# Routed blocks of the first half of the tokens moved ahead in both expert stages, and gate and up biases folded into a plane of the activations

## The chip, the cores and the metric

One core of a Trainium2 chip runs the whole program: TensorE (PE), VectorE (DVE), ScalarE (ACT), GpSimd (POOL) and SyncE (SP, which here only issues DMAs). The metric is the time of one execution on the device in microseconds, the median of several runs.

## What is computed

Four layers over the same 2048 tokens of 128 features, each a token mixer and then a feed-forward part. What matters here are the two expert layers, the first and the last, with two of the experts chosen for every token. Cut from the reference of the last one:

```python
d2 = jnp.sum(xs * xs, -1, keepdims=True) + jnp.sum(centroid * centroid, -1)[None, :] - 2.0 * (xs @ centroid.T)
w, sel = jax.lax.top_k(jnp.sqrt(jnp.maximum(d2, 1e-12)), 2)      # 8 experts
w = jax.nn.softmax(w, axis=1)
for e in range(8):                                                # Wg, W1: 128 x 342, W2: 342 x 128
    h = silu(xs @ Wg[e] + bg[e]) * (xs @ W1[e] + b1[e])
    out = out + we[:, e:e + 1] * (h @ W2[e] + b2[e])
```

`xs` is layernormed without gain or bias, so the sum of a token's 128 features is 0. The first expert layer has 7 routed experts and a shared one that all tokens pass, of width 352, without biases; its router is a plain product. All weights are float32; every product is made of three (high x high, high x low, low x high parts).

## The kernel before

**Stages.** The program is a row of stages with a barrier of all engines between them (`Stage.release`, L165): attention of layer 0, experts of layer 0 (184.8 to 384 us of the profile), attention and `selected_ffn` of layer 1, the same of layer 2, and a last stage (944.8 to the end) that holds the channel attention of layer 3 and its experts. Both expert stages are made by `experts`, the last with `by_distance` true. Tokens lie in 16 tiles of 128, four tiles to a run, four runs.

**Routing.** For each run the stage normalises x (`stats`, `norm`), makes router scores (`router`, `score`), picks two experts for each token (`one_hot`), and numbers the rows of every expert with matmuls of ones (`ranks` on PE, `spot` on DVE): this gives each of a token's two copies a row in `rows` in DRAM, where every expert has its own region. `send` on POOL writes the rows there with indirect DMAs (L1200), two to a tile, eight to a run, 64 in the two stages; all count on one semaphore, `rows_sent`. When all four runs are through, the event `map` makes the block table: PE counts the rows of each expert (L1879), and DVE's `block_table` (L1438 to L1459) turns this into a list of blocks of 128 rows, 38 in the first stage and 39 in the last, each with its expert and its place in `rows`. SP waits for all of `rows_sent` and for the table, reads one entry per block (L1156) and loads the block into one of 8 buffers `yb` (L1159).

**Slots.** A block is worked off in slots that overlap: PE transposes the block two slots ahead (`turn`, L1782), makes gate and up (`gate_up`: L1793, L1794, L1797, each for gate and for up, and in the last stage L1796 for the biases), transposes h (`turn_h`, L1808) and multiplies by the down weights (`down`: L1820, L1821, and L1824 for the down bias). ACT makes silu and the high parts, DVE the product and the low parts, POOL adds the result's rows into `acc` in DRAM (L1207). A slot has 19 matmuls in the last stage and 16 in the first. `work` is the order of the blocks: in the first stage shared tiles 0 to 13, routed blocks 0 to 37, shared tiles 14 and 15; in the last stage only routed blocks. What stands between the slots, and in which order, is a list written by hand that all engines walk through: `shared_first_events` and `mixed_events`. In the last stage all of the channel attention (events that begin with c_) and the routing stand ahead of the first slot.

**Biases of the last stage.** SP zeroes a tile `bias` of 128 x 6496 from DRAM (L2858, 3248 KB) and then places the high and low parts of all biases in its first two partitions; a matmul against a tile of ones in those partitions adds them (L1796, L1824).

**Weights of the last stage.** `load_experts` is called by `load_last` at the end of SP's work in `selected_ffn` of layer 2: gate and up weights of the 8 experts, 128 partitions (L908), three DMAs of down weights (L911: twice 128 partitions, and the rest of 342 rows, 86), then the zeros of `bias`. In the last stage ACT copies them to their high parts and DVE takes the low ones (event `split`, 2 + 2 + 4 experts behind steps 4, 5 and 6 of the list).

## Time and profile before

| | us |
|---|---|
| median of 3 runs | 1178.87 |
| lowest and highest | 1174.91, 1188.52 |
| profiled execution | 1187.66 |
| its span in the profile | 1185.9 |
| its mean granted clock of TensorE | 0.902 of full speed |
| PE busy | 955.9 (81%) |
| DVE, ACT, POOL busy | 719.0, 572.6, 463.9 |
| experts of layer 0 | 184.8 to 384 |
| last stage | 944.8 to 1185.9 |
| its stream of routed slots | 1056.5 to 1160.3 |

The profile shows one execution. A row of a timeline gives the start, the busy time, the engine and line, out<-in by the program's names, and in brackets how long the engine was idle before it and who released it. "SPq" are DMA issues of SP, with the time that the issue took SP, not the transfer. In a row of stretches come the stretch, its length, then for PE, PE's weight loads, DVE, ACT and POOL the busy time with the number of instructions, the granted clock of TensorE as a share of full speed, the busy share of the core's 16 DMA engines and what they moved.

### The profile page before, as it was taken

What the parts mean: (1) busy time and instruction counts of PE and PEld (TensorE: products, weight loads), DVE (VectorE), ACT (ScalarE), POOL (GpSimd) and SP (SyncE); (2) the same over time, 40 slices, a digit from 0 to 9 for tenths busy, and PEclk for the clock granted to TensorE, in tenths of its full rate; (3) what the DMA queues carried; (4) which work ended last, traced back from release to release, by engine and by line L of the source; (5) the groups of instructions that cost most, each with busy time, mean ns of one, the idle gap of its engine ahead of it and who ended that gap; (6) DMA issues with size and microseconds to landing.
All of it is one profiled execution on the core that took longest, in us unless ns stands there. A gap on an engine that the chain in (4) does not pass through costs nothing. (4 is left out here: it accounts for less than half of the span.)

```text
span 1185.9 us, 24279 instructions
## 1 busy us (share of the span) xinstructions
PE 955.9 (81%) x8086; PEld 754.2 (64%) x8101; DVE 719.0 (61%) x1952; ACT 572.6 (48%) x1193; POOL 463.9 (39%) x528
## 2 busy tenths in 40 slices
PE   6899884769993888897789999999997775139990
PEld 5566664769993655555666677767676654139990
DVE  4678645556665767773657666676635556735554
ACT  2577651325553466764444544454432533325552
POOL 1266664533444221211341333343443515733332
PEclk8899995779996999999999999999998887559995
DMA  8121110111212021111400101111113600111113
GB/s 283 49 66 50 50 52 10 35 43 43 55 45 76 26 68 56 56 57 40 139 19 2 32 9 37 38 37 38 38 38 91 237 2 18 33 40 49 53 44 107
DMA packets 80904, 67.05 MB, mean 57 GB/s; under 512 B 6753, under 2 KB 73592, under 8 KB 80402
## 3 DMA queue, kind: packets, MB, share of 16 engines
q1 hardware_dynamic: 76274, 57.04, 16.9%
q0 software_dynamic: 4512, 8.47, 2.2%
q8 instruction: 70, 1.15, 0.4%
q14 instruction: 48, 0.39, 0.1%
HBM read 39.30 MB, written 26.58 MB: 56 GB/s over the span
## 5 line engine op out<-in xcount | busy, mean ns | idle before, releaser
L454 DVE TENSOR_REDUCE a_rowmax<-a_banks 128x4 f32<-128x1024 f32 (+1 forms) x112 | 136.8, 1222 | 64.2 <-PE a_banks L721 28.1
L2314 POOL TENSOR_TENSOR a_both<-a_probs 128x512 f32<-128x512 f32 x64 | 86.2, 1347 | 159.9 <-ACT a_probs L2539 159.9
L576 ACT ACTIVATE a_probs<-a_banks 128x1024 f32<-128x1024 f32 x112 | 114.9, 1026 | 59.9 <-PE a_banks L707 47.2
L1207 POOL DMA_INDIRECT acc<-m_result,m_yb x77 | 75.5, 981 | 141.3 <-DVE m_result L1498 74.4
L2539 ACT ACTIVATE a_probs<-a_banks 128x1024 f32<-128x1024 f32 x64 | 65.6, 1025 | 88.5 <-PE a_banks L2598 88.5
L1607 ACT ACTIVATE m_gate<-m_banks 128x352 f32<-128x352 f32 (+1 forms) x93 | 42.9, 462 | 99.3 <-PE m_banks L1797 97.5
L2445 DVE TENSOR_REDUCE a_rowmax<-a_banks 128x4 f32<-128x1024 f32 x64 | 78.0, 1219 | 13.4 <-PE a_banks L2575 13.4
L1200 POOL DMA_INDIRECT rows<-m_yrow,m_idx x64 | 65.7, 1027 | 51.4 <-issue 21.8
L2612 PE MATMUL a_banks<-a_probs,a_V 128*64 128x256 f32 x512 | 69.4, 392 | 0.6 <-ACT a_craw L2528 0.6
L1478 DVE TENSOR_TENSOR m_h<-m_banks,m_gate 128x342 f32<-128x342 f32 (+1 forms) x55 | 28.5, 517 | 66.4 <-ACT m_gate L1607 59.9
L1820 PE MATMUL m_banks<-e_down,m_hT_hi 128*128 (+2 forms) x231 | 63.6, 344 | 1.0 <-DVE m_result L1498 1.0
L360 POOL TENSOR_SCALAR_AFFINE_SELECT a_probs<-a_probs 128x512 f32<-128x512 f32 (+1 forms) x48 | 38.5, 803 | 64.9 <-ACT a_probs L576 64.8
L749 PE MATMUL a_banks<-a_probs,a_V 128*32 128x256 f32 x720 | 58.4, 396 | 6.8 <-ACT a_raw L564 6.3
L1793 PE MATMUL m_banks<-e_gu_hi,m_y_hi 128*128 x154 | 56.7, 368 | 2.8 <-issue 0.8
L707 PE MATMUL a_banks<-a_QT,a_KT 25*128 25x256 f32 x384 | 48.5, 327 | 12.2 <-DVE a_rowmax L454 10.9
L1484 DVE TENSOR_TENSOR m_hT_lo<-m_banks,m_hT_hi 128x384 fp32r<-128x384 f32 x93 | 51.1, 550 | 4.6 <-ACT m_hT_hi L1613 4.2
L1821 PE MATMUL m_banks<-e_down,m_hT_lo 128*128 (+2 forms) x231 | 51.4, 223 | 0.0
L707 PEld LDWEIGHTS a_banks<-a_QT,a_KT 25*128 25x128 f32 x384 | 29.7, 184 | 33.9 <-issue 20.1
L1797 PE MATMUL m_banks<-e_gu_hi,m_y_lo 128*128 x154 | 50.1, 326 | 0.0
L1808 PE MATMUL m_banks<-ident,m_h 128*128 128x128 f32 (+2 forms) x279 | 48.2, 284 | 2.3 <-DVE m_hT_lo L1484 2.1
L1794 PE MATMUL m_banks<-e_gu_lo,m_y_hi 128*128 x154 | 50.0, 325 | 0.0
L721 PE MATMUL a_banks<-a_KT,a_QT 24*128 24x256 f32 x384 | 48.8, 332 | 0.9 <-ACT a_KT L588 0.9
(378 smaller groups left out, 2812.1 us busy)
## 6 DMA issues: line engine op xcount, KB each, us to landing
rows<-fill SPq DMA_DIRECT2D x16, 520.0 KB, 4.5
a_factor<-recip_rows SPq DMA_DIRECT2D x28, 256.0 KB, 4.8
rows<-fill SPq DMA_DIRECT2D x15, 455.0 KB, 4.2
m_yb<-rows SPq DMA_DIRECT2D x77, 65.0 KB, 1.8
f_expert<-in_experts SPq DMA_DIRECT2D x16, 257.5 KB, 2.9
m_parts<-acc SPq DMA_DIRECT2D x16, 256.0 KB, 4.9
bias<-in_bias_zero SPq DMA_DIRECT2D x1, 3248.0 KB, 20.7
e_gu_lo<-in_gu SPq DMA_DIRECT2D x1, 2736.0 KB
```

The lines of the kernel that those rows point to most:

```text
L454: nc.vector.reduce_max(o, src, AX).then_inc(rowmax_ready, 1)
L576: nc.scalar.activation(probs[h][:, k, :, :], ps[:, 4:6, :], ACT.Exp, scale=SCALE).then_inc(exp_done, 1)
L707: last = mm(ps[:, 4 + x_, b * SEQ:(b + 1) * SEQ], kk[rows, 2 * gp + b, kt * P:(kt + 1) * P], q[rows, 2 * gp + b, :], start=True, stop=True)
L749: last = mm(o[:, 0:SEQ], v, probs[h][:, b // 2 + (0 if causal else 2 * kt), jj, (b % 2) * SEQ:(b % 2 + 1) * SEQ], start=kt == 0, stop=kt = ...
L1200: nc.gpsimd.indirect_dma_start(rows.rearrange("n p c -> (n p) c"), bass.IndirectOffsetOnAxis(idx[:, c:c + 1], 0), yrow[k][:, r * RT + t, : ...
L1207: nc.gpsimd.indirect_dma_start(acc.rearrange("k n d -> (k n) d"), bass.IndirectOffsetOnAxis(yb[b % YB][:, P:P + 1].bitcast(U32), 0), resul ...
L1793: mm(o, y_hi[i % 3][:, :], gu_hi[:, s], start=True, stop=False)
L1820: mm(both, hT_hi[i % 2][0:r, c, :], part[0:r, c, :, :], start=c == 0, stop=False)
L2314: nc.gpsimd.tensor_tensor(both[u % 4][:, :, :], p[:, :, 0, :], p[:, :, 1, :], ALU.add).then_inc(both_ready, 1)
L2445: nc.vector.reduce_max(rowmax[i1 % 2][:, :, j, :, n].rearrange("p t h -> p h t"), ps[:, b:b + 2, :].rearrange("p h (t k) -> p h t k", t=T) ...
L2539: nc.scalar.activation(probs[u % 4][:, :, :, :].rearrange("p h t q -> p h (t q)"), ps[:, 4:6, :], ACT.Exp, scale=SCALE).then_inc(exp_done, 1)
L2612: last = mm(ps[h * D64:(h + 1) * D64, 6, 0:SEQ], V[i % 3][:, kt, j, :], probs[b][:, h, kt, :], start=kt == 0, stop=kt == T - 1)
```

## The change

**Early blocks.** `rows_sent` becomes two semaphores, for runs 0 and 1 and for runs 2 and 3. After run 1's ranks the counts so far are known; DVE's new event `early` makes a table of the first `early_blocks(layer)` blocks, 10 in the first stage and 9 in the last, of those blocks that are full with rows of the first half of the tokens. The event `map` (`late_table`) makes the table of the others, from the counts of all and what the early ones took. SP loads the early blocks after the first semaphore and the early table, the others after the second of each. The count matmuls stand in `ranks` of runs 1 and 3 now. In the first stage the order is shared 0 to 9, routed 0 to 9, shared 10 to 13, routed 10 to 37, shared 14 and 15, and `early` stands behind `router` 2; in the last stage `early` stands behind step 5 of the list, and `map` behind the fourth slot entry. The buffers `yb` and `result` grow from 8 and 4 to 12 each.

**Bias plane.** Since the features of a normalised token sum to 0, its last feature is minus the sum of the others, and the product with a weight matrix is that of 127 features with the matrix less its last row. So feature 127 of the sent rows is set to 1.0, row 127 of the gate and up weights holds the biases, and from every other row the last row is subtracted. This takes away the two L1796 matmuls of a slot, and adds eight tensor_tensor of 128x684 on POOL (`less_last`), a tile `last_row` of 128 x 5472 that is loaded from DRAM (127 copies of the last rows, and zeros), and a DMA of the biases into partition 127. `bias` keeps the down biases alone: 128 x 1024. The events of ACT's copies (`high`) and of DVE's differences (`split`) are now apart and each is placed by itself in the list. ACT's table for silu is loaded at `gap` 3.

```diff
@@ load_experts
-    eng.dma_start(w["gu_lo"][:, :, :].bitcast(F32), src_gu[0:n, :, :].rearrange("e p f -> p e f")).then_inc(w["loaded"], 16)
+        eng.dma_start(w["gu_lo"][0:P - 1, :, :].bitcast(F32),
+                      src_gu[0:n, 0:P - 1, :].rearrange("e p f -> p e f")).then_inc(w["loaded"], 16)
+        eng.dma_start(w["gu_lo"][P - 1:P, :, :].bitcast(F32), bias_gu).then_inc(w["loaded"], 16)
+        eng.dma_start(w["last_row"][:, :, :], copies.rearrange("p (e f) -> p e f", e=n)).then_inc(w["loaded"], 16)
@@ expert_weights
-    w["parts"] = 16 + 16 * FC
+    w["parts"] = (16 if n < NE else 48) + 16 * FC
@@
+def early_blocks(layer):
+
+    return -((ROUTED[layer] * (P - 1) - TOKENS) // P)
@@ mixed_events
-    events = [("c_stats", 0), ("c_norm", 0)]
-    splits = {4: [0, 1], 5: [2, 3], 6: [4, 5, 6, 7]}
+    events = [("c_stats", 0), ("less_last", 0), ("less_last", 1), ("c_norm", 0), ("high", 0), ("high", 1)]
+    highs = {("c_zn", 0): [2, 3], ("norm", 0): [4, 5], ("norm", 1): [6, 7]}
+    splits = {("c_norm", 1): [0, 1], ("c_shift", 0): [2, 3], ("c_shift", 1): [4], ("c_shift", 2): [5], ("c_shift", 3): [6],
+              ("score", 3): [7]}
+    less_last = {("c_stats", 1): [2, 3, 4, 5], ("c_out", 0): [6, 7]}
...
+        if k == 5:
+            events += [("early", 0)]
+    events += [("send", RUNS - 1, 3)]
+    slots = range(-2, W + 2)
+    return events + [("slot", s) for s in slots[:4]] + [("map", 0)] + [("slot", s) for s in slots[4:]]
@@ experts
-            work = [("shared", t) for t in range(14)] + [("routed", b) for b in range(NB)] + [("shared", 14), ("shared", 15)]
+            work = ([("shared", t) for t in range(FIRST_SHARED)] + [("routed", b) for b in range(EARLY)]
+                    + [("shared", t) for t in range(FIRST_SHARED, 14)] + [("routed", b) for b in range(EARLY, NB)]
+                    + [("shared", 14), ("shared", 15)])
@@ SP
-            sp.wait_ge(rows_sent, 16 * 2 * TILES)
-            sp.wait_ge(map_ready, 1)
+            sp.wait_ge(rows_sent[0], 16 * TILES)
+            sp.wait_ge(early_map, 1)
             own_wait(sp, st.sp_waited)
             for b in range(NB):
+                if b == EARLY:
+                    sp.wait_ge(rows_sent[1], 16 * TILES)
+                    sp.wait_ge(late_map, 1)
+                    own_wait(sp, st.sp_waited)
@@ POOL
+                if kind == "less_last":
+                    pool.wait_ge(w["loaded"], w["parts"])
+                    raw_gu, _, _ = raw_parts(w, layer, r)
+                    nc.gpsimd.tensor_tensor(raw_gu, raw_gu, w["last_row"][:, r, :], ALU.subtract).then_inc(less_last, 1)
@@ DVE
+            def early_table():
+                then(nc.vector.memset(step[:, :], float(TILES)))
+                then(nc.vector.reduce_sum(count[:, :], more[:, :, :], AX))
+                block_table(0, EARLY, 0.0, early_map)
+                then(nc.vector.tensor_scalar(taken[:, :], last_of[:, :], float(EARLY), None, ALU.min))
+                nc.vector.tensor_copy(done[:, 0:1], taken[:, 0:1])
+                then(nc.vector.tensor_tensor(done[:, 1:NE], taken[:, 1:NE], taken[:, 0:NE - 1], ALU.subtract))
@@ ACT
-                act.wait_ge(w["loaded"], w["parts"])
...
+                act.wait_ge(less_last, e + 1)
@@ PE, gate_up
-                    if by_distance:
-                        mm(o, bias_one[:, :], biases[:, e, s], start=False, stop=False)
@@ PE, slots
+                    if r == -2 and by_distance:
+                        pe.wait_ge(spot_ready, RUNS)
-                    if r == first_routed - 1:
+                    if r == first_early - 1:
...
-                        pe.wait_ge(map_ready, 1)
+                        pe.wait_ge(early_map, 1)
+                        own_wait(pe, pe_waited)
+                    if r == first_late - 1:
+                        pe.wait_ge(late_map, 1)
@@ load_last
-            load_experts(sp, 3, a["gu3"], a["down3"], w3)
+            load_experts(sp, 3, a["gu3"], a["down3"], w3, (a["gu_last"], a["bias_gu"]))
             sp.dma_start(g.bias[:, :].bitcast(F32), a["bias_zero"]).then_inc(g.bias_zeroed, 16)
```

SP at the end of `selected_ffn` of layer 2 and the start of the last stage, before (e_gu_lo: gate and up weights, e_down: down weights, m_bias_raw: the biases of the last stage):

```order
339 L1972 DMA f_expert<-in_experts 128x515
340 L908 DMA e_gu_lo<-in_gu 128x8x684
341 L911 DMA e_down<-in_down 128x8x128 x2
342 L911 DMA e_down<-in_down 86x8x128
343 L2858 DMA bias<-in_bias_zero 128x6496
344 L1924 UNCONDITIONAL_BRANCH
345 L1144 UNCONDITIONAL_BRANCH
346 L1147 DMA m_bias_raw<-in_bias 32x203
347 L1151 DMA bias<-m_bias_hi 1x32x203
```

And after, at the same place:

```order
339 L2045 DMA f_expert<-in_experts 128x515
340 L913 DMA e_gu_lo<-in_gu 127x8x684
341 L915 DMA e_gu_lo<-in_bias_gu 1x5472
342 L916 DMA e_last_row<-in_gu_last 128x5472
343 L919 DMA e_down<-in_down 128x8x128 x2
344 L919 DMA e_down<-in_down 86x8x128
345 L2931 DMA bias<-in_bias_zero 128x1024
346 L1997 UNCONDITIONAL_BRANCH
347 L1178 UNCONDITIONAL_BRANCH
348 L1181 DMA m_bias_raw<-in_bias 32x32
```

The load of gate and up has 127 partitions in place of 128, two loads stand behind it, and the zeros are 128x1024 in place of 128x6496.

PE at the start of the last stage's slots, after the change (m_chosen: the choices of all runs, m_yb: a loaded block, m_y_hi and m_y_lo: the parts of its transpose):

```order
3108 L1844 MATMUL m_banks<-m_chosen,m_ones 128x8 x4
3109 L1857 MATMUL m_banks<-ident,m_yb 128x128 x2
3110 L1906 TENSOR_LOAD m_block_map
3111 L1906 ISA x2
3112 L1868 ISA
3113 L1868 MATMUL m_banks<-e_gu_hi,m_y_hi 128x342
3114 L1869 REGISTER_ALU
3115 L1869 MATMUL m_banks<-e_gu_lo,m_y_hi 128x342
3116 L1870 MATMUL m_banks<-e_gu_hi,m_y_lo 128x342
```

Before, the same place had L1796 between L1794 and L1797 for gate and again for up.

DVE in the last stage, after the change, behind the choice of run 3's experts (m_top_atf: the experts chosen; e_gu_lo and e_down: the split of one expert; m_step to m_block_map: the early table):

```order
1207 L1420 CAST m_top_atf<-m_top_at 128x8
1208 L1341 TENSOR_TENSOR e_gu_lo<-e_gu_lo,e_gu_hi 128x684
1209 L1342 TENSOR_TENSOR e_down<-e_down 128x2x128
1210 L1343 TENSOR_TENSOR e_down<-e_down 86x128
1211 L1515 MEMSET m_step 1x8
1212 L1516 TENSOR_REDUCE m_count<-m_more 1x8
1213 L1498 TENSOR_TENSOR m_upto<-m_before,m_count 1x64
1214 L1499 TENSOR_REDUCE m_last_of<-m_upto 1x8
1215 L1500 TENSOR_TENSOR m_past<-m_number_f,m_last_of 1x72
1216 L1505 TENSOR_REDUCE m_of_block<-m_past 1x9
```

Before, two splits stood here, four more behind them ahead of the slots, and the whole table behind those; now one split and the early table stand here, and the late table stands between slots.

## Rows read from the trace of the kernel before

**Rows 1.** A stretch of the last stage: busy us by engine, granted clock, DMA share, GB/s.
```profile
1080.00:1150.00 70.00, 70.00 (x525) 69.21 (x525) 40.32 (x112) 37.69 (x110) 26.90 (x28) 1.00 0.19 52
```

**Rows 2.** TensorE's timeline: start, busy us, line, tiles, idle before and its releaser.
```profile
1034.79 0.27 PE L1879 MATMUL m_banks<-m_chosen,m_ones 128*128 128x8 bf16 x4 [2.26 <-DVE m_spot_f L1427]
1054.49 0.47 PE L1782 MATMUL m_banks<-ident,m_yb 128*128 128x128 f32 x1 [19.43 <-DMA m_yb<-rows]
...
1056.54 0.65 PE L1793 MATMUL m_banks<-e_gu_hi,m_y_hi 128*128 x1 [0.34 <-issue]
```

**Rows 3.** The chain of waits, last stage: start, us, what.
```profile
1049.23 2.40 DMA rows<-m_yrow,m_idx
...
1066.19 0.15 PE m_banks L1796
...
1066.61 0.33 PE m_banks L1808 x3
...
1147.70 0.33 PE m_banks L1808 x3
```

**Rows 4.** TensorE's timeline, first stage, at its first routed slots.
```profile
254.47 0.33 PE L1782 MATMUL m_banks<-ident,m_yrow 128*128 128x128 f32 x1 [1.80 <-issue]
...
261.82 0.45 PE L1782 MATMUL m_banks<-ident,m_yb 128*128 128x128 f32 x1 [3.57 <-DMA m_yb<-rows]
```

**Rows 5.** POOL's timeline, last stage.
```profile
948.12 1.02 POOL L1188 TENSOR_TENSOR m_c_in_rstd<-m_c_in_var,minus_half 128x4 f32<-128x4 f32 x1 [2.40 <-DVE m_c_in_var L1284]
...
962.66 1.01 POOL L1188 TENSOR_TENSOR m_c_in_rstd<-m_c_in_var,minus_half 128x4 f32<-128x4 f32 x1 [9.19 <-DVE m_c_in_var L1284]
...
1022.81 0.96 POOL L1200 DMA_INDIRECT rows<-m_yrow,m_idx  x1 [0.30 <-issue]
```

**Rows 6.** VectorE's timeline, first stage and last.
```profile
217.76 0.53 DVE L1478 TENSOR_TENSOR m_h<-m_banks,m_gate 128x352 f32<-128x352 f32 x1 [2.66 <-ACT m_gate L1607]
...
249.76 0.27 DVE L1438 TENSOR_TENSOR m_more<-m_banks,m_limit_f 1x128 f32<-1x128 f32 x1
...
253.62 0.16 DVE L1459 TENSOR_SCALAR m_block_map<-m_of_block 1x38 int32<-1x38 f32 x1
...
1028.45 0.87 DVE L1296 TENSOR_TENSOR e_gu_lo<-e_gu_lo,e_gu_hi 128x684 fp32r<-128x684 f32 x1
...
1031.09 0.28 DVE L1390 TENSOR_TENSOR m_one_hot<-w_moe,m_top_atf 128x32 bf16<-128x32 f32 x2
```

**Rows 7.** Stretches of the first stage.
```profile
261.80:266.50 4.70, 4.67 (x21) 4.61 (x21) 1.16 (x4) 1.56 (x5) 0.00 (x0) 0.50 0.27 61
275.00:355.00 80.00, 77.73 (x556) 73.50 (x555) 49.68 (x137) 45.09 (x139) 33.74 (x35) 1.00 0.19 51
```

**Rows 8.** A group of the page: line, op, shape, count, busy us, mean ns.
```profile
L2314 POOL TENSOR_TENSOR a_both<-a_probs 128x512 f32<-128x512 f32 x64 | 86.2, 1347 | 159.9 <-ACT a_probs L2539 159.9
```

**Rows 9.** Stretches of the two weight loads: last columns clock, DMA share, GB/s.
```profile
24.00:27.00 3.00, 3.00 (x12) 2.21 (x12) 2.18 (x7) 0.00 (x0) 1.45 (x3) 0.50 1.22 266
922.00:925.00 3.00, 2.47 (x15) 2.02 (x14) 1.82 (x10) 2.05 (x7) 2.07 (x3) 1.00 1.02 405
930.00:935.00 5.00, 3.57 (x18) 2.78 (x18) 3.67 (x15) 2.70 (x7) 4.17 (x7) 1.00 0.14 40
939.00:944.00 5.00, 4.91 (x44) 4.71 (x42) 0.68 (x1) 1.58 (x4) 2.63 (x4) 0.99 1.01 437
```

**Rows 10.** SP's timeline: DMA issues, us that each took SP.
```profile
914.78 0.43 SPq L908 DMA_DIRECT2D e_gu_lo<-in_gu  x1
915.27 11.09 SPq L911 DMA_DIRECT2D e_down<-in_down  x3
926.41 8.78 SPq L2858 DMA_DIRECT2D bias<-in_bias_zero  x1
```

**Rows 11.** All engines at the start of the last stage.
```profile
944.83 0.17 POOL L1176 IOTA m_place<- 128x32 int32 x1 [2.84 <-POOLq L165]
```

**Rows 12.** DMA issues of the page: KB each.
```profile
e_gu_lo<-in_gu SPq DMA_DIRECT2D x1, 2736.0 KB
```

More of the change, by code:

```diff
@@ L951 @@
 TOKENS = TILES * P
+FIRST_SHARED = 10
 ROW = P + 2
-BIAS = NE * (2 * F_EXP[3] + P)
+BIAS = NE * P
 BIAS_ROWS = 32
@@ L979, in shared_first_events @@
               ("send", 0, 2), "slot", ("router", 1), ("stats", 3), ("send", 0, 3), ("score", 1), ("norm", 2), "slot",
-              ("gap", 1), ("one_hot", 1), "slot", ("spot", 1), ("share", 1), ("send", 1), ("router", 2), "slot",
-              ("score", 2), ("norm", 3), "slot", ("gap", 2), ("one_hot", 2), "slot", ("spot", 2), ("share", 2),
+              ("gap", 1), ("one_hot", 1), "slot", ("spot", 1), ("share", 1), ("send", 1), ("router", 2), ("early", 0),
+              "slot", ("score", 2), ("norm", 3), "slot", ("gap", 2), ("one_hot", 2), "slot", ("spot", 2), ("share", 2),
               ("send", 2), ("router", 3), "slot", ("score", 3), "slot", ("gap", 3), ("one_hot", 3), "slot",
@@ L988, in mixed_events @@
 def mixed_events(W):
-    events = [("c_stats", 0), ("c_norm", 0)]
-    splits = {4: [0, 1], 5: [2, 3], 6: [4, 5, 6, 7]}
+    events = [("c_stats", 0), ("less_last", 0), ("less_last", 1), ("c_norm", 0), ("high", 0), ("high", 1)]
[3 more added lines that the diff above has]
+    less_last = {("c_stats", 1): [2, 3, 4, 5], ("c_out", 0): [6, 7]}
+    extra = (("less_last", less_last), ("high", highs), ("split", splits))
     for k in range(RUNS + 3):
@@ L998, in mixed_events @@
                 ("send", d, 2)]
-        events += [e for e in step if 0 <= e[1] < RUNS]
-        events += [("split", e) for e in splits.get(k, [])]
-    events += [("send", RUNS - 1, 3), ("map", 0)]
-    return events + [("slot", s) for s in range(-2, W + 2)]
+        for e in step:
+            if 0 <= e[1] < RUNS:
+                events += [e] + [(name, s) for name, at in extra for s in at.get(e, [])]
+        if k == 5:
[3 more added lines that the diff above has]
+    return events + [("slot", s) for s in slots[:4]] + [("map", 0)] + [("slot", s) for s in slots[4:]]
 def experts(nc, g, layer, key, w, mix=None, bias=None, out=None):
@@ L1043, in experts @@
         count = st.sb("count", [1, NE])
+        before = st.sb("before", [1, NE, NE])
         upto = st.sb("upto", [1, NE, NE])
-        last_of = st.sb("last_of", [1, NE])
+        last_of, taken, done, step = (st.sb(n, [1, NE]) for n in ("last_of", "taken", "done", "step"))
         past = st.sb("past", [1, NB, NE])
-        of_block = st.sb("of_block", [1, 4, NB])
+        of_block = st.sb("of_block", [1, 2, NB])
         block_map = st.sb("block_map", [1, 2, NB], I32)
@@ L1101, in experts @@
                  "fn_ready", "x_done", "pe_waited"))
+        rows_sent = [st.sem(f"rows_sent{k}") for k in range(2)]
         block_loaded = [st.sem(f"block_loaded{k}") for k in range(YB)]
@@ L1126, in experts @@
                    ("combine", 3), ("shift", 2), ("residual", 1), ("shift", 3), ("residual", 2), ("residual", 3)]
-        split_at = {e[1]: n + 1 for n, e in enumerate(e for e in events if e[0] == "split")}
         bank = 4 if by_distance else 7
@@ L1461, in low_y, with late_table @@
+            def late_table():
+                nc.vector.tensor_scalar(step[:, :], done[:, :], -1.0, float(TILES), ALU.mult, ALU.add)
+                then(nc.vector.reduce_sum(count[:, :], more[:, :, :], AX))
+                nc.vector.tensor_tensor(step[:, 0:NE - 1], step[:, 0:NE - 1], done[:, 1:NE], ALU.add)
+                then(nc.vector.tensor_tensor(count[:, :], count[:, :], done[:, :], ALU.subtract))
+                block_table(EARLY, NB, done[:, 0:1], late_map)
             def low_y(i):
@@ L1579, in _, with high @@
             nc.scalar.preload_act_table(ACT.Exp if by_distance else ACT.Silu)
-            def split(e):
+            def high(e):
                 r = rows_of[2]
@@ L1681, in _ @@
                         nc.scalar.activation(th[r % 2][:, :], gap[r % 2][:, :], ACT.Tanh, scale=0.5).then_inc(th_ready, 1)
-                if kind == "split":
-                    split(r)
-                if kind == "map" and by_distance:
+                if kind == "high":
+                    high(r)
+                if kind == "gap" and r == RUNS - 1 and by_distance:
                     nc.scalar.preload_act_table(ACT.Silu)
@@ L1769, in ranks @@
                               stop=a == G - 2)
+                if r in (HALF - 1, RUNS - 1):
+                    for q in range(r + 1):
+                        last = mm(counted, ones[:, :], chosen[q][:, :], start=q == 0, stop=q == r)
                 last.then_inc(rank_ps, 1)
@@ L1875, in _ @@
                     ranks(r)
-                if kind == "map":
-                    pe.wait_ge(spot_ready, RUNS)
-                    for q in range(RUNS):
-                        last = mm(counted, ones[:, :], chosen[q][:, :], start=q == 0, stop=q == RUNS - 1)
-                    last.then_inc(count_ps, 1)
                 if kind == "slot":
-                    if r == first_routed - 1:
+                    if r == -2 and by_distance:
+                        pe.wait_ge(spot_ready, RUNS)
+                    if r == first_early - 1:
                         if by_distance:
```

106 lines of the change are left out of this document (64 added, 42 removed).

## The prediction

> **What bounds the kernel now.** I read the page first: TensorE is busy for 81% of the span, but that is a mean over stages with different limits, so the views by stretch decide. In the stream of routed slots of the last stage, 1080 to 1150, TensorE is busy for 70.00 of 70 us at the full clock [rows 1]: every matmul there is time. Ahead of that stream it waits. Its own timeline [rows 2] shows 19.43 us idle before the first transposes of `m_yb`, released by the DMA from `rows`, and the chain of waits [rows 3] says what that DMA waited for: the last of POOL's indirect sends of run 3 (start 1049.23), 2.40 us until its rows had landed. The first stage has the same gap in small: 3.57 us before 261.82, behind 1.80 us in which the block table is made [rows 4].
>
> **Early blocks, last stage.** POOL's sends come eight to a run. Run 1's last starts at 1022.81 [rows 5]; with the 2.40 us to landing of the chain, `rows_sent[0]` is complete at 1025.2. The early table stands on VectorE behind the scores of run 3. At that place stand two splits before, from 1028.45 to 1031.09, 1.32 us each [rows 6]. After, it is one split and fifteen small operations, the first twelve of them up to the map. The whole table of the first stage, thirteen operations up to its map, took 4.0 us (249.76 to 253.78, same rows); the early one works on 9 blocks, and I take 3.0, with 2.4 and 4.0 as bounds. So the early map is there at 1028.45 + 1.32 + 3.0 = 1032.8. From the landing of the sends (1049.23 + 2.40 = 1051.63) to TensorE's first transposes at 1054.49, SP's reads and the load took 2.86 us, so block 0 is there at 1035.7. TensorE waits as well for `spot` of run 3, done near 1034.8, where its count matmuls start; the small operations slip it by less than 1. First turn at 1035.8, first gate matmul 2.05 later, as before (1054.49 to 1056.54), hence 1037.8: a gain of 18.7 us (bounds 16 to 20).
> The second half of the sends ends as before, and its first block can be in SBUF when block 0 was, at 1054.5. It is wanted nine slots of 2.25 us behind the first, its gate matmuls at 1058 and its transposes one to two slots sooner, 1054 to 1057. That is close, and I charge 0.3.
>
> **Bias plane.** Two of nineteen matmuls of a slot go. In a full stretch each of them (L1796) moves the chain on by 0.15 to 0.16 us [rows 3]. The pace: from the transposes at 1066.61 to those at 1147.70 it is 81.09 us for 32 slots, 2.534 each; less 0.31 is 2.22. The bound from the other side is the first stage, whose slots have no such matmul: 556 matmuls in 80 us at 16 a slot are 35 slots, 2.287 each with their gaps and with 352 columns in place of 342 [rows 7]. I take 2.25: 39 x 0.284 = 11.1 us (9.7 to 12.2), and 0.5 more for the first two slots, at the half clock, where each step is twice as long.
>
> **Late tables.** They stand in the stream of slots now. In the first stage the table cost TensorE 1.80 us of idling, and it goes on doing so. In the last stage it stood where TensorE idled anyway; now I charge the same 1.8 there, bounds 0 and 3.7 (the whole table less a slot's slack).
>
> **First stage.** The 3.57 us stall should go, since ten early blocks stand before the late ones, and with it part of the half clock: in the stretch behind it the granted clock is 0.50 for 4.7 us [rows 7], 2.3 us lost, and about 1 more before the stall; I give half of it, 1.65. The early table takes 3 us of VectorE near a gap of 2.66 (before 217.76, [rows 6]): 0.5 lost, and as much again where shared blocks meet the later runs of the router. Gain 3.57 + 1.65 - 1.0 = 4.2, bounds 1 to 7.
>
> **What the plane adds on POOL.** Eight subtractions of 128 x 684. The nearest row has 1347 ns for 128 x 512 [rows 8], 2.6 ns an element, so 1.80 us each. Two stand behind the first `c_in_rstd`, the next four have the gap of 9.19 us before 962.66 [rows 5], two come later: hidden, 0 to 0.2. `high` and `split` only move into idle places of ScalarE and VectorE. All this holds if the weights are in SBUF by 949.
>
> Sum so far: 4.2 + 18.7 + 11.1 + 0.5 - 1.8 - 0.3 = 32.4 us less.
>
> **The load of the weights.** This term decides, and it is of the other sign. Before, the gate and up weights come in one DMA over 128 partitions; now it covers 127 (127x8x684 in SP's rows), 127 x 8 x 684 x 4 bytes = 2.78 MB. Look at what the number of partitions does in the trace [rows 9]. While the 128-row transfer runs, the 16 DMA engines are busy at a share of 1.02 and move 405 GB/s; so they do for `bias_zero`, 128 rows, at 437. Between them stands the down third with 86 rows: 5 us at a share of 0.14, with 40 GB/s. 0.14 of 16 engines is about two, and 86 is 2 x 43. Its twin in the first stage has 96 rows with the same 512-byte runs, and there the share is 1.22 to the end. So a transfer is dealt out to a number of engines that divides its rows, and 127 is prime: one engine. If it were dealt out over the 8 experts, the 86-row load would have had 8 engines and a share of 0.5.
> The Trainium skill says this outright in "DMA: Bandwidth & Descriptors", section "Why a DMA increments its semaphore by 16 and not by 1": a DMA of a hardware queue uses the largest number of engines up to 16 that divides the slowest dimension of both sides, and it lists 127 partitions as 1. The trace agrees, with its share of 0.14 for 86 rows; by this rule the load costs the 103 us worked out below, by even spreading nothing.
> One engine moves 405/16 = 25.3 GB/s: 2.78 MB take 110 us. Bounds: 437/16 = 27.3 gives 102, and 40/2 = 20 gives 139. What is queued behind on the same ring waits: the bias row about 0.9, last_row 2736 KB (as much as [rows 12]) at 405 GB/s 6.9, the two downs of 512 KB 3.4, the 86-row one 352 KB at 40 GB/s 8.8. Together 130 us from about 917 (issue at 914.78, with the last of `f_expert` ahead of it): all is loaded at 1047.
> Who waits for that? SP itself. Its three issues of L911 took it 11.09 us and that of `bias_zero` 8.78, until 935.19, when the 86-row transfer ends [rows 9, 10]: SP doesn't come past a transfer that is still being worked off. The next stage began at 944.8 for all engines together, behind a barrier (L165) that SP belongs to [rows 11]. So the barrier opens at 1047 to 1048 and the stage shifts by 103 us; bounds 93 (fast engine) and 132 (slow one). Nothing hides it, since every engine stands at that barrier; less_last then finds its data at once.
>
> Result: 1187.66 + 103 - 32.4 = 1258.3 for the profiled execution (span 1185.9 and 1.8 around it). It is 8.8 slower than the median of the runs, 1178.87; against that it is 1249.5, forecast 1249.
>
> **The rivals.**
> A. The transfer spreads over many engines after all. For it: the bytes moved are the same, and the 128-row slices show a load that is through in about 10 us. Against it: the 5 us at 0.14. Over 16 engines it lasts 7 us, and only the gains are left: 1178.87 - 32.4 = 1146.5, faster. This is the one that turns my sign, and from this point: with n engines the stage shifts by 110/n - 7 us (103 for one), which is less than the 32.4 from three engines on. Chance 0.10.
> B. The transfer is slow, but SP hands it over and goes on; the stage starts at 944.8. Then the first less_last stands on POOL at 949.1 (948.12 + 1.02, [rows 5]), and behind it in POOL's order all further powers; the others run dry for want of `c_in_rstd` of run 1. Shift 1047 - 949.1 = 97.9: 1244. SP's 8.78 us speaks against it. Chance 0.15.
> C. The engine runs at 20 GB/s, as the 86-row load's two do: 29 us more, 1278. The shorter runs of that load speak against it. Chance 0.13.
> D. The slow load as forecast, but the early blocks bring half, since late blocks come late and tables stall the slots: 16 less of gain, 1265. Chance 0.08.
> The forecast itself 0.52; 0.02 are left for a spreading over three engines, which ends within 1% of the time before.
>
> **Chances and range.** B, C and D are slower too: 0.52 + 0.15 + 0.13 + 0.08 = 0.88 for slower by over 1%. A gives 0.10 for faster. Within 1%, about what a measurement of this kernel can tell from no change: 0.02. The low end takes the fast engine (10 less), full gains (6 less) and an overlap of last_row and the downs with the long transfer, on the other engines (up to 10 less and then some): 1212 with room for two of these being larger than I see. The high end takes C with a part of D: 1284. It leaves A outside.
>
> **What the changed profile would show.** A DMA share near 0.06 with about 25 GB/s for 100 us after 917, TensorE idle beside it, one of SP's issues about as long, and the last stage's first row at 1040 to 1050. Then the smaller terms: first gate matmul 93 us behind the stage's start (before: 112), slots of 2.25 us, no 3.57 us stall in the first stage. I am wrong if the share stays near 1 in that load: then the last stage starts at 945 and the time is near 1146.

## The result, and the profile after

The changed kernel takes 1267.57 us (median of 4 runs, 1264.19 to 1273.59), the kernel before beside it 1179.64. The ratio is 1.074, 95% interval 1.066 to 1.082: 88 us slower. The profiled execution took 1264.19 (span 1261.9), 76.5 more than the profiled one of before; the rest of the difference is that the latter was 8 us above its median and this one 3 below its own.

SP's timeline (start, us that the issue took SP), against [rows 10]:

```profile
899.32 0.34 SPq L913 DMA_DIRECT2D e_gu_lo<-in_gu  x1
899.70 101.18 SPq L915 DMA_DIRECT2D e_gu_lo<-in_bias_gu  x1
1000.93 0.36 SPq L916 DMA_DIRECT2D e_last_row<-in_gu_last  x1
1001.33 21.98 SPq L919 DMA_DIRECT2D e_down<-in_down  x3
1023.34 8.34 SPq L2931 DMA_DIRECT2D bias<-in_bias_zero  x1
```

The load over 127 partitions (L913) is handed over in 0.34 us. The next issue, a single row, takes SP 101.18 us: it stands behind that load until 1000.88. Before, the longest of these rows was 11.09 us, for three issues. The load itself lasts longer than SP is held: its 1016 packets of 2736 bytes (one row of one expert, 684 floats) run from 900.9 to 1015.6 in the trace, 114.7 us, so SP came past it 14.7 us before its end. The stretches (busy us by engine, then granted clock, share of the 16 DMA engines, GB/s), against [rows 9]:

```profile
940.00:960.00 20.00, 0.00 (x0) 0.00 (x0) 0.00 (x0) 0.00 (x0) 0.00 (x0) 0.50 0.06 25
1002.00:1008.00 6.00, 0.00 (x0) 0.00 (x0) 0.00 (x0) 0.00 (x0) 0.00 (x0) 0.50 0.97 365
1020.00:1025.00 5.00, 0.00 (x0) 0.00 (x0) 0.00 (x0) 0.00 (x0) 0.00 (x0) 0.50 0.07 25
1025.00:1030.00 5.00, 0.00 (x0) 0.00 (x0) 0.00 (x0) 0.00 (x0) 0.00 (x0) 0.50 0.14 42
```

While the long load runs, the share is 0.06, one sixteenth, with 25 GB/s. The compute engines first finish their own work of the stage, POOL at 926.1 (106.69 us before 1032.76); from 930 on all of them stand at the barrier, and the clock has fallen to the lower of its two levels. When `last_row` is handed over the rate is back for some us. It falls to one engine again, since that one has the end of the long load left, until 1015.6, and after that nine packets of 21888 bytes one after the other, until 1022.9: the bias row and a sixteenth of the 128 rows of `last_row`. Of the stretches shown, 1020 to 1025 (0.07) is the end of this. Then come the 86 rows, with two (0.14). The last stage starts at 1032.76.

Its start and what follows on POOL and VectorE:

```profile
1032.76 0.16 POOL L1214 IOTA m_place<- 128x32 int32 x1 [106.69 <-POOLq L165]
...
1036.99 3.22 POOL L1260 TENSOR_TENSOR e_gu_lo<-e_gu_lo,e_last_row 128x684 f32<-128x684 f32 x2
...
1038.60 2.46 DVE L1334 TENSOR_SCALAR m_parts<-x,m_c_in_mv,m_c_in_rstd 128x128 f32<-128x128 f32 x4
...
1043.62 6.40 POOL L1260 TENSOR_TENSOR e_gu_lo<-e_gu_lo,e_last_row 128x684 f32<-128x684 f32 x4
1043.68 6.42 DVE L1334 TENSOR_SCALAR m_parts<-x,m_c_in_mv,m_c_in_rstd 128x128 f32<-128x128 f32 x4 [1.12 <-POOL m_c_in_rstd L1226]
```

The columns are start, busy time, line and tiles. Two subtractions took POOL 3.22 us and the next four 6.40. Read the rows of VectorE between them: four tensor_scalar of 128x128 that took 1.11 and 1.12 us before (next fence, kernel before) now take 2.46 and 6.42, and the second four take just as long as POOL's four subtractions beside them.

```profile
949.17 1.11 DVE L1288 TENSOR_SCALAR m_parts<-x,m_c_in_mv,m_c_in_rstd 128x128 f32<-128x128 f32 x4 [1.21 <-POOL m_c_in_rstd L1188]
...
953.50 1.12 DVE L1288 TENSOR_SCALAR m_parts<-x,m_c_in_mv,m_c_in_rstd 128x128 f32<-128x128 f32 x4 [1.12 <-POOL m_c_in_rstd L1188]
```

TensorE at the first slots, against [rows 2], and the stretches of full slots in both stages, against [rows 1, 7]:

```profile
1133.80 0.45 PE L1857 MATMUL m_banks<-ident,m_yb 128*128 128x128 f32 x1 [1.27 <-DMA m_yb<-rows]
...
1135.84 0.65 PE L1868 MATMUL m_banks<-e_gu_hi,m_y_hi 128*128 x1 [0.33 <-issue]
...
1145.62 0.33 PE L1857 MATMUL m_banks<-ident,m_yb 128*128 128x128 f32 x1 [1.43 <-DVE m_y_lo L1533]
```

```profile
255.00:335.00 80.00, 78.36 (x566) 74.79 (x564) 50.91 (x142) 45.84 (x143) 30.72 (x32) 1.00 0.16 45
1160.00:1230.00 70.00, 67.67 (x504) 65.12 (x503) 43.47 (x119) 40.81 (x119) 29.21 (x30) 1.00 0.18 48
```

The wait of 19.43 us is 1.27. A new one of 1.43 us stands at 1145.62, behind the late table. In the last stage's slots TensorE is busy 67.67 of 70 us, not 70.00. The chain of waits (start, us), against [rows 3], has the pace:

```profile
1169.22 0.33 PE m_banks L1881 x3
...
1216.54 0.33 PE m_banks L1881 x3
```

That is 47.32 us for 20 slots, 2.366 each, against 2.534.

Where the time went, by stage, each number the distance between the starts of two stages in the timelines of the two profiled executions (us):

| part | before | after | difference | forecast |
|---|---|---|---|---|
| ahead of the first stage | 184.8 | 181.8 | -3.0 | 0 |
| first expert stage | 200.3 | 186.1 | -14.2 | -4.2 |
| attention 1 and ffn 1 | 224.8 | 226.9 | +2.1 | 0 |
| attention 2 | 288.8 | 288.8 | 0 | 0 |
| ffn 2, up to the start of the last stage | 46.1 | 149.2 | +103.1 | +103 |
| last stage up to its first gate matmul | 111.7 | 103.1 | -8.6 | -18.7 |
| slots and the rest | 129.4 | 126.1 | -3.3 | -9.5 |
| sum | 1185.9 | 1262.0 | +76.1 | +70.6 |

### The profile page after: what moved, and what is told of

It is laid out like the page before. It is cut to its first block and busy times, and to the rows that moved or that the text cites. A ratio compares the mean times of both kernels' runs of the same rounds, so it can differ in the third digit from the quotient of the medians.

```text
span 1261.9 us, 24112 instructions
## 1 busy us (share of the span) xinstructions
PE 943.2 (75%) x8012; PEld 739.0 (59%) x8027; DVE 735.6 (58%) x1995; ACT 573.1 (45%) x1193; POOL 474.4 (38%) x536
## 5 line engine op out<-in xcount | busy, mean ns | idle before, releaser
L1245 POOL DMA_INDIRECT acc<-m_result,m_yb x77 | 75.5, 980 | 111.7 <-DVE m_result L1569 57.6
L2612 ACT ACTIVATE a_probs<-a_banks 128x1024 f32<-128x1024 f32 x64 | 65.6, 1025 | 88.5 <-PE a_banks L2671 88.5
```

The costliest lines, as they stand in the source:

```text
L1245: nc.gpsimd.indirect_dma_start(acc.rearrange("k n d -> (k n) d"), bass.IndirectOffsetOnAxis(yb[b % YB][:, P:P + 1].bitcast(U32), 0), resul ...
L2612: nc.scalar.activation(probs[u % 4][:, :, :, :].rearrange("p h t q -> p h (t q)"), ps[:, 4:6, :], ACT.Exp, scale=SCALE).then_inc(exp_done, 1)
```

## The experiments

All ratios are to the kernel before, run beside on the same chip, with their 95% interval.

**The load, taken out of the change.** `one_load`: the biases are put into row 127 of the array in DRAM, and it is loaded in one piece.

```diff
-        eng.dma_start(w["gu_lo"][0:P - 1, :, :].bitcast(F32),
-                      src_gu[0:n, 0:P - 1, :].rearrange("e p f -> p e f")).then_inc(w["loaded"], 16)
-        eng.dma_start(w["gu_lo"][P - 1:P, :, :].bitcast(F32), bias_gu).then_inc(w["loaded"], 16)
+        eng.dma_start(w["gu_lo"][:, :, :].bitcast(F32),
+                      src_gu[0:n, :, :].rearrange("e p f -> p e f")).then_inc(w["loaded"], 16)
```

> The changed kernel, with the gate and up weights loaded as one transfer over 128 partitions again (the biases are put into row 127 of the array in DRAM beforehand); all else as changed. If the 127-row transfer is the cause, the last stage starts about 103 us sooner and the time is 1160 to 1169 us, 12 to 18 under the kernel before. If the new wait on the loads, or the 2736 KB of last_row behind them, is the cause, it stays above 1230.

Measured: 1185.37 us, ratio 0.996 (0.992 to 1.000). SP's timeline:

```profile
918.45 0.43 SPq L913 DMA_DIRECT2D e_gu_lo<-in_gu  x1
918.93 0.58 SPq L915 DMA_DIRECT2D e_last_row<-in_gu_last  x1
919.55 15.37 SPq L918 DMA_DIRECT2D e_down<-in_down  x3
934.96 9.51 SPq L2930 DMA_DIRECT2D bias<-in_bias_zero  x1
```

The same bytes, `last_row` among them, are handed over in 26.0 us (918.45 to 944.47), and the last stage starts 45.9 us after ffn 2, as before (46.1). So neither `last_row` nor the new wait on the loads moves the start of the stage; the 127 rows do. But the time is not the forecast 1160 to 1169: against before there is almost no gain left. Where the other gains are is what the next experiments ask.

**The load, put into the kernel before.** `before_127`: 127 rows and 1 row, and nothing else of the change.

```diff
-    eng.dma_start(w["gu_lo"][:, :, :].bitcast(F32), src_gu[0:n, :, :].rearrange("e p f -> p e f")).then_inc(w["loaded"], 16)
+        for p0, p1 in ((0, P - 1), (P - 1, P)):
+            eng.dma_start(w["gu_lo"][p0:p1, :, :].bitcast(F32),
+                          src_gu[0:n, p0:p1, :].rearrange("e p f -> p e f")).then_inc(w["loaded"], 16)
```

> The kernel before, whose load of the gate and up weights is cut into 127 rows and 1 row, and nothing else. One engine for 127 rows: 101 us more for that load, as in the changed kernel, less what lay free ahead of the barrier: 1262 to 1280 us. If the transfer were spread anyway and the changed kernel lost its time elsewhere: 1178 to 1184.

Measured: 1282.23 us, ratio 1.079 (1.071 to 1.088), and on its SP:

```profile
911.77 101.56 SPq L912 DMA_DIRECT2D e_gu_lo<-in_gu  x2
...
1013.37 12.37 SPq L916 DMA_DIRECT2D e_down<-in_down  x3
1025.79 8.41 SPq L2863 DMA_DIRECT2D bias<-in_bias_zero  x1
```

One edit of the load makes the kernel before 93 us slower; taking it out brings the changed one from 88 us over the kernel before to 4 under, 92. Both directions agree: the load is the whole loss. The load's packets run for 111.5 us here, at 25.1 GB/s, and SP came past them 12 us before their end.

**Other numbers of rows.** `rows_112_15`: the change as it is, its 127 rows in two transfers.

```diff
-        eng.dma_start(w["gu_lo"][0:P - 1, :, :].bitcast(F32),
-                      src_gu[0:n, 0:P - 1, :].rearrange("e p f -> p e f")).then_inc(w["loaded"], 16)
+        for p0, p1 in ((0, 112), (112, 127)):
+            eng.dma_start(w["gu_lo"][p0:p1, :, :].bitcast(F32),
+                          src_gu[0:n, p0:p1, :].rearrange("e p f -> p e f")).then_inc(w["loaded"], 16)
```

> The changed kernel as it is, but with its 127 rows loaded as two transfers, of 112 and of 15 rows. By the divisor rule they get 16 and 15 engines: level with one_load, within 1%, some 80 us under the changed kernel. If a load that leaves out partition 127, or one that is cut in parts, is slow for another reason, it stays above 1230 us.

Measured: 1190.78 us, ratio 1.005 (1.003 to 1.008). The same 127 rows in another cut, and the ratio falls from 1.074 to 1.005: it is the number of rows in one transfer, not the missing partition, nor the cut. (The Trainium skill, "DMA: Bandwidth & Descriptors", section "Why a DMA increments its semaphore by 16 and not by 1", has the rule: the largest number up to 16 that divides the slowest dimension of both sides. The shares agree for 128, 96, 86 and 127 rows, 1.02, 1.22, 0.14 and 0.06, and the time for 112 and 15.)

**The subtractions on POOL.** `no_subtract` leaves them out but for one column of each expert.

```diff
-                    nc.gpsimd.tensor_tensor(raw_gu, raw_gu, w["last_row"][:, r, :], ALU.subtract).then_inc(less_last, 1)
+                    nc.gpsimd.tensor_tensor(raw_gu[:, 0:1], raw_gu[:, 0:1], w["last_row"][:, r, 0:1], ALU.subtract).then_inc(less_last, 1)
```

> As one_load, but POOL's eight subtractions of the last row take one column each in place of 684 (the weights then lack the subtraction in the other columns). If the subtractions hold up VectorE (m_parts took 6.42 us beside them and 1.12 without), the channel attention ends 8 to 10 us sooner: 1151 to 1159. If the late start of the stage, cold and after a long rest, made that part longer, one_load has lost it already and this one gives under 2 us more.

Measured: 1177.79 us, ratio 0.992 (0.988 to 0.996). Its median is 8 us under one_load's, ten executions each on the same chip, but the intervals overlap, so I look at the profile. VectorE's four tensor_scalar, beside POOL's small ones:

```profile
950.20 1.11 DVE L1333 TENSOR_SCALAR m_parts<-x,m_c_in_mv,m_c_in_rstd 128x128 f32<-128x128 f32 x4 [0.67 <-POOL m_c_in_rstd L1225]
...
953.96 1.14 DVE L1333 TENSOR_SCALAR m_parts<-x,m_c_in_mv,m_c_in_rstd 128x128 f32<-128x128 f32 x4 [1.13 <-POOL m_c_in_rstd L1225]
```

They are at 1.11 and 1.14 again. The part ahead of the slots is 93.3 us long, against 103.5 in one_load and 111.7 before. So the early blocks, with the splits in their new places, gain 18.4 us there, and the subtractions take 10.2 of them back. The Trainium skill states the mechanism in "SBUF — State Buffer", section "Who interferes with whom": GpSimd and VectorE share a pair of ports, and while one of them holds it for an instruction the other is blocked. The trace agrees (6.42 us beside 6.40). Two rows of the kernel before told of it, sends of POOL beside VectorE's splits, where a send usually takes 0.96 us:

```profile
1030.45 1.76 POOL L1200 DMA_INDIRECT rows<-m_yrow,m_idx  x1 [0.30 <-issue]
...
1037.99 2.00 POOL L1200 DMA_INDIRECT rows<-m_yrow,m_idx  x1 [0.30 <-issue]
```

**The subtractions on VectorE.** `sub_dve_tuned` is one_load with the event moved to VectorE, and two, two and two of them behind c_norm 1, c_out 0 and c_out 1.

```diff
-    less_last = {("c_stats", 1): [2, 3, 4, 5], ("c_out", 0): [6, 7]}
+    less_last = {("c_norm", 1): [2, 3], ("c_out", 0): [4, 5], ("c_out", 1): [6, 7]}
...
-                    nc.gpsimd.tensor_tensor(raw_gu, raw_gu, w["last_row"][:, r, :], ALU.subtract).then_inc(less_last, 1)
+                    nc.vector.tensor_tensor(raw_gu, raw_gu, w["last_row"][:, r, :], ALU.subtract).then_inc(less_last, 1)
```

> As one_load, with the eight subtractions on VectorE (0.86 us each, 6.9 us in all) and three pairs of them put behind c_norm 1, c_out 0 and c_out 1, where VectorE idled before. If the two engines keep each other out of the memory, one engine alone does better: 3 to 7 us under one_load. If the subtractions cost by their own work on the path, it is level with it, within 2.

Measured: 1180.50 us, ratio 0.994 (0.990 to 0.998), a median 5 us under one_load's with overlapping intervals; the part ahead of the slots takes 97.3 us. Work that VectorE does itself, put where it idled, costs 4.0 there, the same work on POOL beside it 10.2. The engine and the places changed together, so the share of each isn't known.

**Each half alone.** `plane_only` makes SP wait for all rows and both tables, and puts the tables and the shared tiles where they were:

```diff
             sp.wait_ge(rows_sent[0], 16 * TILES)
             sp.wait_ge(early_map, 1)
+            sp.wait_ge(rows_sent[1], 16 * TILES)
+            sp.wait_ge(late_map, 1)
...
-    return events + [("slot", s) for s in slots[:4]] + [("map", 0)] + [("slot", s) for s in slots[4:]]
+    return events + [("map", 0)] + [("slot", s) for s in slots]
...
-FIRST_SHARED = 10
+FIRST_SHARED = 14
```

> As one_load, with nothing early: SP waits for all rows and both tables, and the tables stand where the old one stood. Slots without their two bias matmuls give 8 to 11 us, the subtractions on POOL take 8 to 10 us of the channel attention: level with the kernel before, within 4 us. And if the stall of 6 to 8 us that one_load shows in its first slots comes from slots that run beside the sends, it is absent here; if it comes from the plane, it is here too.

`early_only` takes the plane out: the biases come by the two L1796 matmuls again, no `last_row`, no subtractions.

```diff
+                    if by_distance:
+                        mm(o, bias_one[:, :], biases[:, e, s], start=False, stop=False)
...
-                act.wait_ge(less_last, e + 1)
```

> As one_load, but without the plane: weights as before, biases by two matmuls a slot, no subtractions; early blocks in both stages. The part of the last stage ahead of its slots is 93 to 95 us long (before 111.7, one_load 103.5); if the stall in the first slots belongs to the overlap with the sends, it is here, and slots and tail take 135 to 142 us (before 129.4): 6 to 12 us under the kernel before. If it belongs to the plane, it is not, and the time is 14 to 19 us under.

Measured: plane_only 1191.60, ratio 1.004 (1.001 to 1.007); early_only 1184.44, ratio 0.998 (0.995 to 1.000). TensorE at the first slots of plane_only, then of early_only:

```profile
1065.57 0.45 PE L1854 MATMUL m_banks<-ident,m_yb 128*128 128x128 f32 x1 [18.39 <-DMA m_yb<-rows]
...
1067.50 0.65 PE L1865 MATMUL m_banks<-e_gu_hi,m_y_hi 128*128 x1 [0.30 <-issue]
```

```profile
1042.02 0.47 PE L1846 MATMUL m_banks<-ident,m_yb 128*128 128x128 f32 x1 [1.30 <-DMA m_yb<-rows]
...
1058.22 0.47 PE L1846 MATMUL m_banks<-ident,m_yb 128*128 128x128 f32 x1 [6.12 <-DVE m_y_lo L1523]
```

plane_only has the old wait back (18.39 us). Its slots and the rest take 122.2 us (1067.50 to the end at 1189.7), 7.2 less than before; ahead of them it is 8.7 longer, the price of the subtractions. The plane as it stands is worth nothing. early_only has 93.9 us ahead of the slots, a gain of 17.8, and then a wait of 6.12 at 1058.22 which before has not, and 139.5 for slots and the rest, 10 more than before. The early blocks, with that wait, are worth 3 us, not the 18.7 forecast for that part, nor the 6 to 12 expected here.

**The first stage in the old order.** `early_last_only`:

```diff
+            if not by_distance:
+                sp.wait_ge(rows_sent[1], 16 * TILES)
+                sp.wait_ge(late_map, 1)
...
-                if b == EARLY:
+                if b == EARLY and by_distance:
...
-FIRST_SHARED = 10
+FIRST_SHARED = 14
```

> As one_load, but the first stage is in the old order (shared tiles 0 to 13, and all routed blocks wait for all rows and both tables). If early blocks gain 4 us there, as the prediction had it, this is 3 to 6 us over one_load; if the gain is eaten by the same kind of stall beside the sends, it is level with it, within 2.

Measured: 1182.98, ratio 0.995 (0.992 to 0.999), level with one_load. In these two the first stage takes 199.7 us, before 200.3: early blocks gain nothing there, in a stage that has the waits shown next. Yet in the changed kernel it took 186.1.

**A wait of ScalarE that nothing explains.** Here is what one_load has in both stages and the changed kernel in neither. ScalarE, then TensorE, of one_load:

```profile
235.96 0.28 ACT L1671 ACTIVATE m_y_hi<-m_banks 128x128 fp32r<-128x128 f32 x1 [1.63 <-remote]
239.53 0.49 ACT L1683 ACTIVATE m_hT_hi<-m_banks 128x384 fp32r<-128x384 f32 x1 [3.29 <-remote]
...
1062.53 0.46 ACT L1677 ACTIVATE m_gate<-m_banks 128x342 f32<-128x342 f32 x1 [7.52 <-issue]
```

```profile
1057.30 0.32 PE L1869 MATMUL m_banks<-e_gu_hi,m_y_lo 128*128 x1
1065.30 0.47 PE L1856 MATMUL m_banks<-ident,m_yb 128*128 128x128 f32 x1 [7.69 <-DVE m_y_lo L1532]
```

The second gate product of the last stage was done at about 1056, and no other wait stands before this m_gate in the program; it starts at 1062.53, after 7.52 us that no engine released ("issue"; in the first stage the releaser is "remote"). Everything stops behind it, TensorE for 7.69 us. In these profiles such a wait of a slot begins only while POOL's sends run: never in the last stage of before or plane_only, whose slots come after the sends; in the first stage of before too (4.67 and 3.12 us, before 242.50 and 254.84). In the last stage one_load, no_subtract, sub_dve_tuned, rows_112_15, early_only and early_last_only have it, 7.1 to 9.7 us long, and it ends 0.2 to 3.3 us after the start of the last send.

Is it the execution, the order or the program? `after_again` is the changed kernel once more, on the chip of the next experiment.

> The changed kernel itself, beside the kernel before once more. It should lie 83 to 95 us over the kernel before, as it did. Its first profile shows no long wait of ScalarE beside POOL's sends, in either stage, where all variants with the short load show 6 to 8 us. If that wait depends on the program, it is absent again; if it depends on the execution or the chip, it can be here.

Measured: 1266.19, ratio 1.071 (1.065 to 1.077). First stage 186.5 us, no such wait. That a second execution lacks it too fits a wait that belongs to the program, but doesn't show it: turn_first, the other program profiled on this chip, has none either. `turn_first` puts, in sub_dve_tuned, the transposes of each slot ahead of its gate matmuls, on three engines:

```diff
-                    if there(r):
-                        gate_up(r, expert_of(r))
                     if there(r + 2):
                         turn(r + 2)
+                    if there(r):
+                        gate_up(r, expert_of(r))
```

> As sub_dve_tuned, and in each slot the transposes of the block two slots ahead stand before the gate matmuls, on all three engines. If the slots without bias matmuls wait for the chain h, y_lo (0.25 us before every second gate matmul), the pace goes from 2.36 to 2.25 us and the time is 3 to 6 us under sub_dve_tuned, 10 to 14 under the kernel before. If the pace is TensorE's own, it is level with sub_dve_tuned, within 2.

Measured: 1156.29, ratio 0.980 (0.976 to 0.984), where sub_dve_tuned has 0.994 on another chip: more than expected, and not for the reason given, since its pace of 2.36 us a slot is sub_dve_tuned's. The wait is gone, the first stage takes 184.0 us, slots and the rest 125.7. Order, or how the program lies in memory? `before_turn_first` has that order and nothing else,

> The kernel before, with nothing of the change, and the transposes ahead of the gate matmuls in each slot, on TensorE, ScalarE and VectorE. If that order by itself takes away ScalarE's long waits beside the sends, the first stage is 12 to 16 us shorter and the time 1162 to 1170 us. If turn_first was quick for another reason (how its program happens to lie), it is level with the kernel before, within 3.

and `tuned_64_64` has the old order and one more DMA instruction on SP.

```diff
-        eng.dma_start(w["gu_lo"][:, :, :].bitcast(F32),
-                      src_gu[0:n, :, :].rearrange("e p f -> p e f")).then_inc(w["loaded"], 16)
+        for p0, p1 in ((0, 64), (64, 128)):
+            eng.dma_start(w["gu_lo"][p0:p1, :, :].bitcast(F32),
+                          src_gu[0:n, p0:p1, :].rearrange("e p f -> p e f")).then_inc(w["loaded"], 16)
```

> As sub_dve_tuned, but its 128-row load is cut into two of 64 rows, 16 engines each: one more DMA instruction of SP, as many as in the changed kernel, and no other difference. If ScalarE's long waits hang on how the program lies, they can vanish with it: 1155 to 1162 us, and a first stage of 184 to 187 us in place of 198. If they hang on the order of the work alone, it is level with sub_dve_tuned, within 3.

Measured: before_turn_first 1196.47, ratio 1.014 (1.006 to 1.021): the order by itself loses. Its pace is 2.64 us a slot where before has 2.53. Neither branch of the expectation came: it has no such wait of ScalarE, and yet its first stage takes 198.0 us. TensorE there waits for the routed rows instead, 7.07 us where before waits 3.57 [rows 4]:

```profile
257.32 0.45 PE L1782 MATMUL m_banks<-ident,m_yb 128*128 128x128 f32 x1 [7.07 <-DMA m_yb<-rows]
```

turn_first, also without the waits and in the same order of a slot, but with early blocks and their 12 buffers, takes 184.0. So where ScalarE's waits are absent the first stage is 14 us shorter with early blocks, 7.07 of them this stall (the rest isn't taken apart); where they are present it is not shorter at all.

tuned_64_64 1157.67, ratio 0.984 (0.976 to 0.992), where sub_dve_tuned has 0.994. ScalarE of sub_dve_tuned, then of tuned_64_64, at the same places:

```profile
240.41 0.49 ACT L1683 ACTIVATE m_hT_hi<-m_banks 128x384 fp32r<-128x384 f32 x1 [3.29 <-remote]
...
1049.10 0.46 ACT L1677 ACTIVATE m_gate<-m_banks 128x342 f32<-128x342 f32 x1 [7.50 <-issue]
```

```profile
1043.29 0.28 ACT L1672 ACTIVATE m_y_hi<-m_banks 128x128 fp32r<-128x128 f32 x1 [1.29 <-PE m_banks L1857]
1047.20 0.46 ACT L1678 ACTIVATE m_gate<-m_banks 128x342 f32<-128x342 f32 x1 [1.59 <-PE m_banks L1870]
```

The first stage takes 184.7 us in place of 198.0, slots and the rest 125.7 in place of 133.3, with the same work in the same order of a slot. So work and order alone don't make the wait. What does is open. One candidate is how the program lies in memory, since one DMA instruction more is the only edit; against it, rows_112_15 and before_127 have more instructions on SP as well and keep the wait. The other is the chip, which was not held fixed: all eight programs profiled on chips 11 and 12 have such waits, none of the four on chips 10 and 3, and sub_dve_tuned (12) and tuned_64_64 (3) never ran on the same one. The kernel before fits this too, with medians of 1189.0 and 1187.2 on chips 12 and 11 and 1181.4 and 1176.7 on 10 and 3. The ratios to it, 0.990 to 0.998 against 0.976 to 0.992, overlap. Both programs on one chip would settle it; no run here does.

## Why the prediction was right

The time, 1267.6, lies in the range of 1212 to 1284, 18.6 above the forecast of 1249; point by point:

- **The load of the weights** was forecast to shift the last stage by 103 us, and shifted it by 103.1. The mechanism (one engine, SP held up, all engines at the barrier) is shown by one_load, before_127 and rows_112_15. The parts were less exact than their sum. The transfer itself took 114.7 us against the forecast 110, at 24.2 GB/s. But SP was let go 14.7 us before its end, after 101, where I had said that SP doesn't come past a transfer that is still being worked off; and from there to the start of the stage it was 32 us (1000.9 to 1032.8), not 20, since the one engine had the end of the load and a part of all that stood behind it to work off alone. That these come to 103.1 us against 103 is luck.
- **Rivals.** A falls with the share of 0.06. B falls: SP did not go on at once, its next issue took 101.18 us, and the stage started at 1032.76, not 944.8. C falls, the rate was 24.2 GB/s. D is half true: the last stage gave 11.9 of its 28.2 us, but not because late blocks came late.
- **Early blocks, last stage:** forecast -18.7, and without the subtractions it is -18.4 (no_subtract) and -17.8 (early_only). The size of that term held. In the changed kernel it was -8.6.
- **What the plane adds on POOL** was the step that failed: "hidden, 0 to 0.2". It cost 10.2 us. I had asked whether POOL was idle at that place, and it was, and sized one subtraction at 1.80 us where it took 1.60; I hadn't asked what VectorE did beside it. The rows that told were in the trace: POOL's sends took 1.76 and 2.00 us beside VectorE's splits, where 0.96 is usual.
- **Bias plane:** forecast 11.1 us from a pace of 2.25; the pace is 2.366, 6.6 us for 39 slots. The term was mis-sized: two matmuls of 0.156 less would be 2.22, but TensorE is no longer the only bound. It is busy 67.67 of 70 us and waits 0.1 to 0.3 us in every second slot, before a gate matmul, for VectorE's `m_y_lo`, 0.08 us a slot on average. The other 0.06 to 0.07 isn't explained. The bound of the first stage was the nearer row; it was given as 2.287 over 35 slots, and 556 matmuls at 16 a slot are 34.75, which makes it 2.30.
- **Late tables:** forecast 1.8; the new wait is 1.43, and in the stretches 1146 to 1150 behind it the granted clock is 0.60 and 0.55, where it had been 1.00. Late blocks never stalled, as forecast.
- **First stage:** forecast -4.2, measured -14.2. The stall for the first routed rows went, as forecast, but its size hangs on ScalarE's waits, which the changed kernel's profiles lack and which the prediction did not reckon with. With them early blocks gain nothing (early_last_only level with one_load, 199.7 us both); without them the stall was 7.07 us, and the stage is 14 shorter with early blocks (198.0 in before_turn_first, 184.0 in turn_first). It takes both, and no run here says what removed the waits.
- **Medians.** The forecast of 1249 took the profiled execution of before at 8.8 above its median and carried the same distance over; the changed kernel's profiled execution lay 3.4 below its own median. 12.2 of the 18.6 us are this.
- **The sum.** The forecast of the profiled difference, 70.6 us against 76.1, is closer than its terms: the last stage gave 16.3 less than forecast, the first stage 10.0 more. That these nearly cancel is luck as well.

Better than both kernels are turn_first, 1156.3 us, and tuned_64_64, 1157.7: the change with a load of 128 rows and its subtractions on VectorE. Their ratios to the kernel before are 0.980 and 0.984. one_load and sub_dve_tuned, with ScalarE's waits, come to 0.996 and 0.994. How much of the difference is the program's and how much the chip's is not shown.

## What to carry to other kernels

Count the partitions of a large DMA: 127 in place of 128 turned loads that held SP for 26 us into 132 (899.32 to 1031.68). Fill the odd row in DRAM, or cut the transfer into pieces, as 112 and 15 rows here. POOL's idle time was not free for new work here, since VectorE worked beside it; look at both. And before a variant is judged by 1 or 2%, look whether a wait that no engine released has come or gone with it, and compare variants on the same chip.

## What was not expected

- ScalarE stands still for 2 to 10 us in some of these profiles while POOL's indirect sends run, with everything it waits for done. Between sub_dve_tuned and tuned_64_64, which differ in one DMA instruction on SP and in the chip, it makes up 13 us in the first stage (198.0 against 184.7) and 7.6 in the last (133.3 against 125.7). Its cause is open.
- Two gains can hang on each other: the first stage is 14 us shorter with early blocks where these waits are absent (198.0 against 184.0), and no shorter where they are present (199.7 both).
- A transfer over one engine goes on costing after SP has come past it: in this trace SP went on 14.7 us before the load's end, what it handed over then was dealt to all engines, and the late one worked off its part alone, until 1022.9, at a share of 0.07.
- VectorE's tensor_scalar of 128x128 waited for POOL's tensor_tensor of 128x684: four that take 1.12 us alone took 6.42.
